# Where SyncE stores the output and loads the residual in an attention kernel's batch loop, and when Pool adds the bias

## What is computed

```python
q = split_heads(x @ w_q)
out_text = merge_heads(sdpa(q, split_heads(text @ w_k), split_heads(text @ w_v)))
out_ip = merge_heads(sdpa(q, split_heads(ip_h @ w_k_ip), split_heads(ip_h @ w_v_ip), mask=mask_ip))
out = (out_text + out_ip) @ w_out + b_out
out = out + x
```

## Time and profile before

| what | value |
|---|---|
| time, median of 3 runs | 588.21 us (580.64 to 588.48) |
| time of the profiled execution | 583.03 us |
| its span in the trace | 581.2 us |
| mean granted TensorE clock | 0.975 |
| busy: TensorE, weight loads, VectorE, ScalarE, Pool | 91%, 65%, 68%, 52%, 28% |
| chain that ended last, by engine | TensorE 40%, DMA 21%, issue 11%, VectorE 10%, SyncE's queue 9%, Pool 5% |
| moved | 111.15 MB, 191 GB/s on average |

### The profile page before, as it was taken

One profiled execution on the slowest core, in us unless ns is written; L12 is line 12 of the kernel. 1 busy time (PEld: TensorE's weight loads), 2 busy tenths in 40 slices (PEclk: granted clock), 3 DMA queues, 4 the chain that ended last, 5 costly groups with the idle time before them and its releaser, 6 DMA issues.

```text
span 581.2 us, 13366 instructions
## 1 busy us (share of the span) xinstructions
PE 531.0 (91%) x3984; PEld 377.4 (65%) x3984; DVE 396.9 (68%) x994; ACT 304.2 (52%) x549; POOL 163.2 (28%) x222
## 2 busy tenths in 40 slices
PE   3899899999998789998999988999889899899993
PEld 2788688788787555665656655656556566566651
DVE  2767442532535779896888988788889789888730
ACT  3542443434441456664665656566556566566660
POOL 9241000000000312423433423234334243242442
PEclk9999899999998979998999999899999999999997
DMA  8978888888979897767557766677578567767111
GB/s 265 373 237 176 268 275 290 291 275 254 296 258 256 226 225 152 169 151 175 156 120 186 188 140 174 131 185 176 116 195 176 132 174 189 150 173 151 35 46 45
DMA packets 96951, 111.15 MB, mean 191 GB/s; under 512 B 17568, under 2 KB 75936, under 8 KB 96928
## 3 DMA queue, kind: packets, MB, share of 16 engines
q1 hardware_dynamic: 96288, 109.58, 70.3%
q0 software_dynamic: 640, 1.28, 1.4%
HBM read 72.22 MB, written 38.60 MB: 191 GB/s over the span
## 4 chain that ended last, share of the span: by engine, by line
PE 40%; DMA 21%; issue 11%; DVE 10%; SPq 9%; POOL 5%; ACT 1%; POOLq 0%; DVEq 0%; ACTq 0%
DMA max_rows<-row_buf 10%; DMA k_stack<-k_parts 9%; PE pv L739 6%; SPq L290 6%; PE score_q L677 6%; PE score_t L725 6%; PE score_t L643 2%; PE score_t L644 2%; PE score_t L645 2%; PE pj L643 2%; PE pj L749 2%; POOL o_turned L394 2%; DVE max_cols L562 2%; PE pj L644 2%; PE pj L645 2%
## 5 line engine op out<-in xcount | busy, mean ns | idle before, releaser
L493 ACT ACTIVATE probs<-score_t 128x512 f32<-128x512 f32 x320 | 176.0, 599 | 142.6 <-PE score_t L725 142.5
L562 DVE TENSOR_REDUCE max_cols<-score_q 128x2 fp32r<-128x496 f32 x320 | 208.8, 654 | 53.9 <-PE score_q L677 53.4
L725 PE MATMUL score_t<-q_stack,k_stack 128*128 128x256 f32 x640 | 152.9, 323 | 0.5 <-ACT probs L493 0.5
L677 PE MATMUL score_q<-k_stack,q_stack 128*128 128x512 f32 x320 | 129.5, 410 | 25.5 <-DMA k_stack<-k_parts 21.9
L725 PEld LDWEIGHTS score_t<-q_stack,k_stack 128*128 128x128 f32 x640 | 112.2, 192 | 57.1 <-issue 34.0
L739 PE MATMUL pv<-probs,v_cur 128*32 128x256 f32 x1920 | 122.7, 389 | 0.9 <-ACT o_all L479 0.9
L394 POOL TENSOR_TENSOR o_turned<-o_turned,inv_cols 128x256 f32<-128x256 f32 x80 | 49.7, 621 | 151.2 <-DVE inv_cols L617 151.2
L739 PEld LDWEIGHTS pv<-probs,v_cur 128*32 128x32 f32 x1920 | 55.0, 110 | 49.7 <-issue 11.0
L677 PEld LDWEIGHTS score_q<-k_stack,q_stack 128*128 128x128 f32 x320 | 61.4, 193 | 31.1 <-issue 13.9
L749 PE MATMUL pj<-wo_sb,o_all 128*128 128x320 f32 x192 | 64.5, 446 | 4.7 <-ACT out_sb L485 2.4
L614 DVE STREAM_TRANSPOSE o_turned<-o_all 128x512 f32<-128x512 f32 x80 | 54.6, 682 | 6.0 <-ACT o_all L479 6.0
(11 more groups left out here) (135 smaller groups left out, 685.5 us busy)
## 6 DMA issues: line engine op xcount, KB each, us to landing
q_stack<-q_parts SPq DMA_DIRECT2D x96, 160.0 KB, 3.4
k_stack<-k_parts SPq DMA_DIRECT2D x192, 80.0 KB, 3.3
v_rows<-v_out SPq DMA_DIRECT2D x32, 320.0 KB, 2.5
v_cur<-v_rows SPq DMA_DIRECT2D x16, 640.0 KB
o_all<-in_ctxT SPq DMA_DIRECT2D x16, 512.0 KB, 5.8
q_parts<-qk_out SPq DMA_DIRECT2D x32, 256.0 KB, 2.5
k_parts<-qk_out SPq DMA_DIRECT2D x32, 248.0 KB, 4.5
q_stack<-aux_rows SPq DMA_DIRECT2D x32, 160.0 KB, 3.7
```

What stands on the lines that cost most here:

```text
L493: nc.scalar.activation(probs[:, slot(u, p), 2 * S * e:2 * S * (e + 1)], score_t[:, 512 * e:512 * e + 512], ACT.Exp, scale=SCALE)\
L562: nc.vector.tensor_reduce(out=max_cols[:, h, t, at:at + 2], in_=both[:, :, 0:TEXT], op=ALU.max, axis=AX.X, negate=True)
L677: mm(score_bank(first, 2 * p + t), q_cols(u, p, t * P, P), k_cols(u, p, 0, 0, 2 * KEYS), start=True, stop=True).then_inc(sq_ready, 1)
L725: last = mm(score_t[:, 512 * e + S * t:512 * e + S * t + S], k_cols(u, p, e, t, P), q_cols(u, p, 0, S), start=True, stop=True)
```

## The change

On SyncE the store of batch b - 2's output and the load of batch b's residual move from the middle of the batch to its end, behind the keys of batch b + 2. On Pool the bias is added to the residual of batch b - 1 in the program for batch b, between normalisations 1 and 2, instead of to that of batch b at its start.

```diff
@@ SyncE, batch(b, u)
                 load_rows(b, u, 1)
                 if there(b, 1):
                     load_stack_k(b + 1, 1 - u, 1)
-                if there(b, -2):
-                    store_out(b - 2)
-                load_residual(b, u)
                 if there(b, 1):
                     need(sp, pv_ready, QUADS * b)
                     load_values(b + 1, 1 - u)
...
                     load_rows(b + 1, 1 - u, 0)
                 if there(b, 2):
                     load_stack_k(b + 2, u, 0)
+                if there(b, -2):
+                    store_out(b - 2)
+                load_residual(b, u)
@@ Pool
+            def add_bias(b, u):
+                pool.wait_ge(xr_loaded[u], 8 * (b - u) + 16)
+                pool.tensor_tensor(x_res[:, u, :, :], x_res[:, u, :, :],
+                                   bias_sb[:, :].unsqueeze(1).broadcast_to([P, OT, D]), ALU.add).then_inc(biased, 1)
             def normalise(b, u):
                 if there(b, -2):
                     pool.wait_ge(biased, b - 1)
                     add_residual(b - 2, u)
-                pool.wait_ge(xr_loaded[u], 8 * (b - u) + 16)
-                pool.tensor_tensor(x_res[:, u, :, :], x_res[:, u, :, :],
-                                   bias_sb[:, :].unsqueeze(1).broadcast_to([P, OT, D]), ALU.add).then_inc(biased, 1)
                 for k in range(QUADS):
+                    if k == 2 and there(b, -1):
+                        add_bias(b - 1, 1 - u)
...
             batches(pool, normalise, tail=False)
+            pool.wait_ge(biased, B - 1)
+            add_residual(B - 2, 0)
+            add_bias(B - 1, 1)
             pool.wait_ge(biased, B)
-            for b in (B - 2, B - 1):
-                add_residual(b, b % 2)
+            add_residual(B - 1, 1)
```

## The result

The change made the kernel slower: a median of 667.25 us (662.61 to 668.69) against 587.88 us (580.64 to 588.48), ratio 1.137 with a 95% interval of 1.126 to 1.147. The profiled execution took 667.66 us, 84.6 us more than that of the kernel before. Forecast were 658 us in a range of 630 to 680.

The account below looks back on a forecast made before the run. A loop through memory nearly as long as TensorE's work was taken as the bound. Batches 2 to 13 at 29.2 us gave +73.7, batch 14 +1.6: +75.3 on 583.0, forecast 658 us, range 630 to 680.

Parts of the forecast that it names:

- The maxima's way: First half's row maxima on SyncE, from their store to the row load: 4.91 us was to become about 2.78.
- Alone this would take away the 21.9 us: SyncE's reordering by itself would remove TensorE's waits for keys, 21.9 us in 15 places, and no more.
- Pool's edit at nothing: Adding the bias one batch later on Pool was costed at nothing, covered by Pool's idleness; bound +1.56 us per batch.
- The stop: TensorE at tile 1's projection, waiting for ScalarE's lift, held until the output's store lands: 5.9 us per batch.
- S: The start of the batch being followed, 387.51 us for batch 8 of the kernel before; times are S + something.
- third rival: Store stuck behind query and key loads for 4.4 us, clock costing 2.5: 30.8 per batch, 678 us; chance 0.13.
- The clock: TensorE at its lower clock after each stop: 2.0 us lost per stop, between 1.7 and 2.5, bound 0.
- Another such gap: TensorE's gap before 205.7 us, clock 0.50 over the next 5 us, read as 2.5 us of full rate lost.
- The first rival: The same stop, but TensorE's clock holds its full level: 12 x 27.2 us for the batches, 634 us; chance 0.17.
- Batch 14: No key loads left there, so the store goes out at 14.6 and the lift ends at 17.4: +1.6 us.
- Faster: Rival: store lands by S + 13.7, before the lift wants it, and the key wait is won: 561 us; chance 0.02.
- no difference: Rival: the change does nothing because the store was last anyway: 583 us; chance 0.03.

Follow-up runs that it names:

- the one with two buffers: The changed kernel with two buffers for out_sb and a semaphore for each, the changed order kept; measured 559.18 us, ratio 0.953 to the kernel before.
- the filled run: The changed kernel with 22 matmuls, results overwritten, put ahead of the projection of tile 1 in batches 2 to 13; 639.09 us, ratio 1.092 to the kernel before.
- the run with 3.2 us: The changed kernel with the output's store moved ahead of the six key loads of the batch's end; 627.99 us, ratio 1.073 to the kernel before.

## Why the prediction was right

**What bounds the kernel.** The loop through memory was the bound: with the store out of the way it shrinks, and TensorE's 21.06 us per batch remain (21.27 on average over the loop), against the 21.33 read from the trace.

**The gain on SyncE.** The maxima's way was forecast to fall to 2.78 us and took 2.77; the wait for keys went to 5.1 us. "Alone this would take away the 21.9 us" comes out nearly, but by partly other terms. It starts from the profiled execution of 583.03 us, and the one with two buffers took 560.18, 22.9 less. (The 29 us between the medians are more because that execution was 5 us below its median.) 21.5 of the 22.9 lie between the starts of batches 2 and 14, where only 17.5 of the 21.9 us of waits stood. The forecast left out two terms. Behind two of the waits TensorE came back at the low clock, and batches 3 and 7 (from 271.21 and 363.45) last 1.6 us longer each, beside their waits. And a batch takes 21.33 us behind a wait and 21.06 without one, 0.27 x 12 = 3.2 us. Together that is 23.9; the run with two buffers itself lies 2.5 us over 12 x 21.06. For the changed kernel, 12 x (21.06 + 6.07 + 2.46) = 355.1 us against 357.2 measured. The values' load was to start some 5 us earlier; it was 3.8.

**Pool's edit at nothing.** Right, by the run with it alone: 0 to +0.9%.

**The stop.** Its steps came out nearly as worked out: store issued at S + 17.92 (forecast 17.9), landing 3.4 us (3.3), TensorE back at S + 21.82 (21.7), 5.6 to 6.5 us of stop with a mean of 6.07 (5.9). ScalarE's twelve waits in the loop are 7.3 to 8.2 us, 92.9 in all (7 to 8, about 90). Taking the key loads' landing, 3.3, over the 2.4 us of a quiet queue gave the right size, but the reason given, six key loads just ahead, is not what the runs show: issued ahead of them, with the query loads in front instead, the store lands no sooner (3.1 to 3.6 us). In batch 14, where neither query nor key loads are issued ahead of it, it is 2.6. What in the traffic around the store costs the extra microsecond stays open. The "longer stop" of the third rival did not occur. By the completion order of the Trainium skill's page "DMA: Bandwidth & Descriptors" (section "Queues, rings and completion order") the landing would be at least 2.8 us. The 3.4 agree, but no run tells that rule apart from plain traffic on the queue.

**The clock.** The mechanism held, its size was low: 2.0 us per stop were taken, 2.46 measured (7.05 - 4.59), 2.36 of it clock by the filled run. With the stop's 0.17 us that were missing too (12 x 0.17 = 2.0) and the 2.0 of batch 14 below, 12 x 0.46 = 5.5 us make up 9.5 of the 9.7 us by which the profiled execution exceeds the forecast. The 2.0 came from rows that are less alike than the prediction says. "Another such gap", before 205.7, is not of the same kind: TensorE had worked little ahead of it, and the clock fell before it ended:

```profile
200.00:203.60 3.60, 1.54 (x6) 0.72 (x4) 2.63 (x8) 1.37 (x3) 0.00 (x0) 1.00 0.96 262
203.60:205.70 2.10, 0.00 (x0) 0.00 (x0) 1.20 (x5) 0.39 (x1) 0.00 (x0) 0.58 0.99 205
```

That leaves one gap of some 2 us with the low level behind it and one without, and there was luck in how near the 2.0 came. The first rival, full clock after the stop, falls with the run that filled it: it is what that run shows, at 639.09 us, and not the changed kernel. The clock granted behind the three stops shown is 0.50 to 0.69; with that agrees what the Trainium skill, "TensorE: Matmul & The Clock Gate", Part 1, says, that the low level is the default. The prediction's "every stop is followed by it" goes too far: behind three of thirteen stops of the run with the store ahead of the key loads the clock stayed at 1.00.

**Batch 14.** +1.6 was forecast. The stop there is 1.91 us, and the low clock follows this one too (6.24 us to the last projection instead of 4.59): +3.6. I had priced this stop without the clock, and that is another 2 us. The clock over the 5 us behind it is 0.66:

```profile
622.80:627.80 5.00, 5.00 (x34) 3.22 (x34) 1.94 (x6) 2.61 (x5) 0.00 (x0) 0.66 0.02 5
```

It need not have come: of the three runs with such a stop, this one and the filled one (1.94 us) have the 6.24, and the one with the store ahead of the key loads has 4.69 (1.84 us).

**Faster, or no difference.** The condition named for "faster", a landing by S + 13.7, is what the store behind the values reaches, and it is faster by 3.7%. The mechanism was priced at 561 us; the run gives 563.42.

## What to carry to other kernels

A transfer moved back in an issuing engine's order is paid for by whoever waits to reuse its buffer: before it is moved behind other waits, look up who waits for its landing, and at what time of the loop. A single buffer fixes a latest place for its store; with that place kept, or a second buffer, the same edit that cost 13.7% gives 3.7 to 4.7%. And a stop of TensorE costs its own length plus what it does at the low clock afterwards, here 40% on top of stops of 6.1 us, and two thirds on average on top of stops of 3.2 us, where single stops were spared.

## What the runs showed of the hardware that was not expected

The price of the clock follows the length of the stop only loosely: on average it was 2.46 us behind stops of 6.1 us (1.6 to 3.0) and 2.1 behind stops of 3.2. Under the same code it varied from stop to stop between 0.1 and 2.9 us in the run with 3.2 us (4.69 to 7.53 us against 4.59), and was 1.65, 1.65 and 0.1 behind three stops of 1.8 to 1.9 us. All twelve stops of 6.1 us were followed by the low level. And 264 needless matmuls made a kernel 28.2 us faster, because they stood where TensorE would have stood still.
